# 13 node slots per tile, layer 0 projected side by side, coefficients of both layers in three column groups, 340 found tiles in layer 1

## The chip, the core and the metric

The kernel runs on one NeuronCore of a Trainium2 chip. Its engines work side by side, each through its own list of instructions, and wait for one another by semaphores: TensorE (PE, with its weight loads PEld) multiplies matrices into PSUM, VectorE (DVE) and ScalarE (ACT) work element by element, GpSimd (POOL) issues the indirect DMAs here, and SyncE (SP) issues the plain ones. The metric is the time of one execution on the device in microseconds, the median of several runs. Lower is better.

## What is computed

Two graph layers over 12500 nodes with 32 features and 200000 edges sorted by destination. Layer 0 mixes, for each edge, the source node's normalized features with nine edge values, through 32 x 32 matrices. Layer 1 mixes with 16 basis matrices whose weights depend on the edge's relation and on an attention value, plus one matrix for the last edge of each node.

```python
edge_index = jnp.stack([src, dst])
h = jnp.maximum(_layernorm(x, axis=-1), 0.0)
x = x + _L0_gnn_ref(h, edge_index, edge_weight1, edge_attr_3, edge_attr_5, L0_gnn_W)
h = jnp.maximum(_layernorm(x, axis=-1), 0.0)
x = x + _L1_gnn_ref(h, ..., src, dst, edge_type_86)
...
nei = jax.ops.segment_sum(a[:, None] * msg, dst, num_segments=N)
h_new = jnp.where((in_deg > 0)[:, None], nei + curr, jnp.zeros_like(nei))
```

Both layers sum their edge messages by destination node. Since the destination sum and the matrices commute, the kernel sums the coefficient-weighted source rows first and multiplies by the matrices afterwards.

## The kernel before

The edges are cut into tiles of 128 (one edge per partition) and the tiles into groups of 12 (`J`), 130 full groups (`FULL`) and a tail of 3 tiles. Each layer runs over the 131 groups once (`edge_sums`, `edge_copies`, `edge_work`, `edge_gathers`, `edge_loads`, one per engine); further passes over everything run only where a tile of 128 edges reaches over more destination nodes than it has slots (`WN`, 14 before).

Source rows reach SBUF (`xg`, four buffers, one per group modulo 4) in two ways. GpSimd gathers most tiles with one indirect DMA each (L564); it may begin the gathers of a group only when the sums of the group four before it are done (`summed`). The last two or three tiles of a group (`NP`, per layer and group) are found by TensorE instead: VectorE writes 0/1 blocks of the wanted row numbers (`block_rows`, L1024), TensorE multiplies them with the whole node table in 14 matmuls (`find_rows`, L636), and VectorE picks the row out of each block (`pick_rows`, L1033 and L1038). A group therefore has 12 minus `NP` gathers. Layer 0 finds 2 tiles in the first 8 groups and 3 after that. Layer 1 finds 2, then alternately 3 and 2, 322 in all.

The sums: VectorE spreads each edge's coefficients over the node slots, `Z` (`spread`, L1095; 9 coefficients in layer 0, 17 in layer 1, times 14 slots). TensorE multiplies each tile's rows with its Z (`sum_edges`, L717), in column groups of 32 (`QS`: three groups of 3 coefficients in layer 0; four groups of 5, 4, 4 and 4 coefficients in layer 1), which write to different partitions of PSUM (`G_ps`). A float32 matmul stands in the trace as two records. ScalarE copies the result to SBUF (`copy_G`, L880, L878).

The projection: in layer 0, `project` (L662) multiplies each half's three chunks with `w0c`, 64 columns wide: 32 columns of sums and 32 of the same minus their mean over the features, which the next layer's normalization uses. In layer 1 there are two steps. `project_in_quarters` (L675) writes the products of five chunks into four column groups, ScalarE copies them (`copy_oT`, L886), and `sum_quarters` (L687) adds the quarters. Then ScalarE copies the result (`copy_o`, L893), TensorE moves it to its place in the window of 128 nodes (`place_rows`, L699), and VectorE adds the window to `aggT` (`add`, L1106). Layer 1 also has attention: one-hot rows on ScalarE (L846, L850) and 36 matmuls (`attention_rows`, L649).

The order on each engine is written out by hand in the functions `step`. On TensorE, a step with new group s finds its first tile, projects group s-2, finds the other tiles, in layer 1 sums the quarters of s-2 and does the attention of s, and then sums the edges of s-1; after the first four tiles of these sums it places s-2. On VectorE a step writes blocks, picks rows and adds the window of s-3, then nodes, the first tile of s, the blocks of its third tile, and spread. On ScalarE it copies G, then (layer 1) one-hots, the quarters, attention, then placing, and last the projected rows. GpSimd does nothing but gathers.

## Time and profile before

| | us |
|---|---|
| three runs | 4622.65, 4632.38, 4634.9; median 4632.38 |
| the profiled execution | 4637.38 |
| its span, first to last instruction | 4635.5 |
| TensorE, busy | 3578.4 (77%) |
| VectorE, busy | 2689.9 (58%) |
| GpSimd, busy | 2301.7 (50%) |
| ScalarE, busy | 1097.0 (24%) |

The time of a matmul record is its start and a modelled end; the runs of records of one line are merged in the timelines. "Idle before" names what ended an engine's wait: an engine and line, "issue" where the profile shows nothing that it waited for, and "remote" for an unknown queue or a signal whose sender had been done for long.

### The profile page before, as it was taken

Reading aid. Unit: us, or ns where it says so; the run is one execution under the profiler, and the core shown is the slowest. Engines: PE = TensorE matmul, PEld = TensorE weight load, DVE = VectorE, ACT = ScalarE, POOL = GpSimd, SP = SyncE. Lnnn points to the kernel's source line nnn. Section 1 sums busy time; section 2 is a strip of 40 time slices with the busy share of each in tenths; the row PEclk is TensorE's granted clock in tenths of the full one; section 3 lists DMA queues with packets and bytes.
Section 4 is the critical chain, followed back from the end, with each engine's and each line's share of the span. In section 5 each row is a group of like instructions: output and inputs, shape, how many; then the busy total and the mean of one; then the engine's idle time right before and its main releaser. Section 6 shows DMA issues by size and latency. Waiting matters only on the chain.

```text
span 4635.5 us, 106735 instructions
## 1 busy us (share of the span) xinstructions
PE 3578.4 (77%) x41254; PEld 3052.1 (66%) x41254; DVE 2689.9 (58%) x3863; ACT 1097.0 (24%) x2563; POOL 2301.7 (50%) x2427
## 2 busy tenths in 40 slices
PE   3788888888888888885677777777777777777777
PEld 2677777777777777775566666666666666666666
DVE  5455555555555555555555665656656665556565
ACT  1111111111111111112233333333333333333332
POOL 5555555555555555553344444544444444445442
PEclk9889988888988989997788888888888888888887
DMA  3111111111111111111122222222222222222221
GB/s 102 21 21 20 20 21 19 20 20 21 20 20 21 20 20 21 21 20 54 35 38 39 38 37 38 40 37 37 37 41 37 38 39 38 37 37 39 39 37 35
DMA packets 216608, 150.09 MB, mean 32 GB/s; under 512 B 121048, under 2 KB 197261, under 8 KB 216079
## 3 DMA queue, kind: packets, MB, share of 16 engines
q0 software_dynamic: 77504, 39.84, 8.9%
q1 hardware_dynamic: 137999, 100.77, 8.8%
q8 instruction: 335, 5.49, 0.5%
q10 hardware_dynamic: 576, 2.40, 0.1%
q14 instruction: 194, 1.59, 0.1%
HBM read 134.58 MB, written 8.22 MB: 31 GB/s over the span
## 4 chain that ended last, share of the span: by engine, by line
PE 38%; issue 13%; another core or an unknown queue 2%; DVE 1%; ACT 1%; ACTq 0%; DVEq 0%
PE ps L636 20%; PE ps L717 7%; PE ps L649 5%; PE ps L675 2%; PE ps L699 1%; PE ps L687 1%; PE ps L599 0%; ACT p_left L846 0%; PE ps L619 0%; DVE room L1095 0%; DVE row_var L969 0%; ACT p_left L886 0%; DVE squares L996 0%; DVE H L966 0%
## 5 line engine op out<-in xcount | busy, mean ns | idle before, releaser
L564 POOL DMA_INDIRECT xg<-h_table,idx x2422 | 2290.8, 946 | 2272.7 <-PE ps L717 1530.1
L636 PE MATMUL ps<-h,blocks 128*128 128x448 f32 x9856 | 2284.3, 388 | 43.3 <-DVE blocks L1024 29.2
L636 PEld LDWEIGHTS ps<-h,blocks 128*128 128x128 f32 x9856 | 1937.9, 202 | 262.8 <-issue 76.6
L1024 DVE TENSOR_TENSOR blocks<-scratch,ps 128x896 fp32r<-128x896 int16 x704 | 761.2, 1082 | 882.8 <-remote 864.7
L717 PE MATMUL ps<-room,xg 128*32 128x42 f32 (+2 forms) x21882 | 699.4, 267 | 301.5 <-issue 297.4
L717 PEld LDWEIGHTS ps<-room,xg 128*32 128x32 f32 x21882 | 579.6, 144 | 429.0 <-issue 412.4
L1033 DVE SCALAR_TENSOR_TENSOR scratch<-ramp_sb,scratch,ps 128x448 f32<-128x448 f32 x704 | 476.4, 677 | 512.1 <-remote 250.7
L649 PE MATMUL ps<-att_tab,p_left 128*128 128x49 bf16 x4689 | 261.2, 200 | 555.3 <-issue 553.7
L1095 DVE TENSOR_TENSOR room<-coef,ps 128x756 f32<-128x756 f32 (+1 forms) x522 | 648.9, 1284 | 4.9 <-DVE ps L1044 0.2
L649 PEld LDWEIGHTS ps<-att_tab,p_left 128*128 128x128 bf16 x4689 | 201.6, 107 | 610.5 <-issue 609.5
L880 ACT ACTIVATE p_left<-ps 96x504 f32<-96x504 f32 (+2 forms) x262 | 168.8, 644 | 1200.8 <-PE ps L717 1200.7
L1038 DVE TENSOR_REDUCE xg<-scratch 128x32 f32<-128x448 f32 x704 | 436.6, 620 | 25.6
L893 ACT ACTIVATE p_left<-ps 84x128 f32<-84x128 f32 (+2 forms) x262 | 64.4, 246 | 1428.9 <-remote 1189.8
L846 ACT ACTIVATE p_left<-rows_b,node_all 128x512 bf16<-128x512 int16 x391 | 251.6, 705 | 48.8 <-PE ps L649 48.8
L699 PE MATMUL ps<-squares,p_left 84*64 84x128 f32 (+1 forms) x1044 | 241.3, 372 | 11.5 <-issue 10.6
L850 ACT ACTIVATE p_left<-p_left 128x1536 bf16<-128x1536 bf16 x131 | 193.5, 1477 | 4.1
L1076 DVE TENSOR_TENSOR coef<-ps,att 128x192 f32<-128x192 f32 x131 | 46.6, 356 | 232.8 <-issue 116.1
L865 ACT ACTIVATE squares<-ramp_sb,place 84x128 f32<-84x128 f32 x522 | 179.2, 391 | 9.7 <-issue 9.7
L1106 DVE TENSOR_TENSOR aggT<-aggT,ps 64x128 f32 (+1 forms) x262 | 74.1, 283 | 179.8 <-PE ps L699 137.2
L699 PEld LDWEIGHTS ps<-squares,p_left 84*64 84x64 f32 (+1 forms) x1044 | 144.4, 166 | 26.0 <-issue 13.0
L878 ACT ACTIVATE p_left<-ps 32x168 f32<-32x168 f32 x131 | 39.2, 300 | 476.9 <-PE ps L717 476.9
L662 PEld LDWEIGHTS ps<-w0c,p_left 96*84 96x84 f32 x1566 | 137.5, 155 | 11.3 <-ACT p_left L880 1.6
(108 smaller groups left out, 1144.5 us busy)
## 6 DMA issues: line engine op xcount, KB each, us to landing
xg<-h_table,idx POOLq DMA_INDIRECT x2422
rows_b<-typ_short SPq DMA_DIRECT2D x130, 258.0 KB
scratch<-q_short SPq DMA_DIRECT2D x260, 96.0 KB
rows_b<-dst_short SPq DMA_DIRECT2D x130, 126.0 KB
coef<-in_edge_dram SPq DMA_DIRECT2D x130, 54.0 KB
att_tab<-p_table SPq DMA_DIRECT2D x393, 8.1 KB
p_table<-room SPq DMA_DIRECT2D x8, 297.0 KB
X<-in_x_dram SPq DMA_DIRECT2D x7, 224.0 KB, 4.3
```

Source lines behind the costliest of these rows:

```text
L564: pool.indirect_dma_start(xg[:, g.q, t - g.s * J, :], None, h_table[n], bass.IndirectOffsetOnAxis(ap=idx[:, t:t + 1], axis=0)).then_inc(L. ...
L636: last = pe.matmul(found_ps[b], blocks[:, b, c, :], h_2[:, a, c], start=(c == 0 and a == 0), stop=(c == NCH - 1 and a == 1))
L649: last = pe.matmul(to, one_hot[:, j, :], att_tab[:, g.b, j // JS, a, :], start=(a == 0), stop=(a == 2))
L699: last = pe.matmul(win_ps[OUT[n]], o_sb[0:w, h, 0:no], R[0:w, g.b, h, :], start=(h == 0), stop=(h == hh - 1), tile_position=(0, OUT[n].start))
L717: last = pe.matmul(bank[q * F:(q + 1) * F, 0:qs[q + 1] - qs[q], j % JH, :], xg[:, g.q, j, :], Z[:, g.b, j, qs[q] * WN:qs[q + 1] * WN], sta ...
L846: act.activation(one_hot[:, js, :].rearrange("p j e -> p (j e)"), rows_b[:, b, js.start * P:js.stop * P], ACT.Abs, bias=node, scale=-1.0). ...
L850: act.activation(one, one, ACT.Relu, bias=1.0, scale=-1.0).then_inc(L.one_hot_set, 1)
L865: act.activation(R[0:w, g.b, h, :], iota_row[0:w, :], ACT.Abs, bias=at, scale=-1.0)\
L1024: dve.tensor_tensor(blocks[:, b], q_b[:, g.b, i, :].unsqueeze(1).broadcast_to([P, NCH, P]), block_ps.unsqueeze(2).broadcast_to([P, NCH, P] ...
L1033: dve.scalar_tensor_tensor(out=picked, in0=iota_row[:, 0:MC].unsqueeze(1).broadcast_to([P, F, MC]), scalar=place_in_block[:, bass.ds(u, 1) ...
L1038: dve.tensor_reduce(xg[:, g.q, j, :], picked, AX_X, ALU.add).then_inc(L.picked, 1)
L1095: dve.tensor_tensor(Z[:, b, js, 0:C * WN].rearrange("p j (c n) -> p j c n", n=WN), coef[:, js, :].unsqueeze(3).broadcast_to([P, k, C, WN]) ...
```

## The change

Tiles get 13 node slots instead of 14, so Z, the sums and all that is copied and projected shrink by a fourteenth. The 17 coefficients of layer 1 go into three column groups of 6, 6 and 5 instead of four, so there are six chunks (the last with two groups) for the projection instead of five. Layer 0 uses the two-step projection of layer 1 (`project_in_quarters`, then ScalarE's `copy_oT`, then `sum_quarters` after the second found tile) with `w0c` 32 columns wide; the centred half is no longer a product of the matmul but is made by VectorE in a new function `centre`, for which `place_rows` of layer 0 waits. In layer 1 two of three groups find 3 tiles, 340 in all.

```diff
-WN = 14
+WN = 13
-NP = [[2 if s < 8 else 3 for s in range(FULL)], [2 if s < 8 else 3 if s == FULL - 1 else 3 - s % 2 for s in range(FULL)]]
+NP = [[2 if s < 8 else 3 for s in range(FULL)], [2 if s < 8 or s == FULL - 2 else [2, 3, 3][s % 3] for s in range(FULL)]]
-QS = [[0, 3, 6, 9, 9], [0, 5, 9, 13, 17]]
-CQ = [3, 5]
-NQ = [3, 4]
+QS = [[0, 3, 6, 9, 9], [0, 6, 12, 17, 17]]
+CQ = [3, 6]
+NQ = 3
+CHUNK = [[3 * F, 3 * F, 3 * F], [3 * F, 3 * F, 3 * F, 3 * F, 3 * F, 2 * F]]
...
-                def project(g):
-                    ...
-                            last = pe.matmul(o_ps[0:w, h, 0:no], G_sb[0:rows, c, h, 0:w], weights[0:rows, c, :],
-                                             start=(c == 0), stop=(c == cq - 1))
...
                     for c in range(cq):
-                        rows, q = (P, c) if c < MQ else (F, 0)
+                        rows, q = CHUNK[n][c], c % MQ
                         last = pe.matmul(oT_ps[q * F:(q + 1) * F, 0:hh * w], weights[0:rows, c, :], G_sb[0:rows, c, 0:hh, 0:w],
-                                         start=(c < MQ), stop=(c > 0), tile_position=(0, q * F))
+                                         start=(c < MQ), stop=(c + MQ >= cq), tile_position=(0, q * F))
...
                 def place_rows(g):
-                    pe.wait_ge(L.o_set, g.order())
+                    pe.wait_ge(L.centred if n == 0 else L.o_set, g.order())
...
                 def step(gs):
                     tiles = gs[0].found_tiles(n) if gs[0] else []
                     find_rows(tiles[0:1])
+                    if gs[2]:
+                        project_in_quarters(gs[2])
+                    find_rows(tiles[1:2])
                     if n == 0 and gs[2]:
-                        project(gs[2])
-                    if n == 1 and gs[2]:
-                        project_in_quarters(gs[2])
-                    find_rows(tiles[1:])
+                        sum_quarters(gs[2])
+                    find_rows(tiles[2:])
                     if n == 1 and gs[2]:
                         sum_quarters(gs[2])
...
                 def step(gs):
                     if gs[2]:
                         copy_G(gs[2])
                     if n == 1 and gs[0]:
                         one_hots(gs[0])
-                    if n == 1 and gs[2]:
+                    if gs[2]:
                         copy_oT(gs[2])
...
+                def centre(g):
+
+                    hh, w = g.halves()
+                    dve.wait_ge(L.o_set, g.order())
+                    wait(dve, L.centred, g.order() - 1)
+                    dve.tensor_reduce(o_sum[0:w, 0:hh], o_sb[0:w, 0:hh, 0:F], AX_X, ALU.add).then_inc(L.o_sum_set, 1)
+                    dve.wait_ge(L.o_sum_set, g.order())
+                    wait(dve, L.placed, g.order() - 1)
+                    dve.scalar_tensor_tensor(out=o_sb[0:w, 0:hh, F:2 * F], scalar=-1.0 / F, op0=ALU.mult, op1=ALU.add,
+                                             in0=o_sum[0:w, 0:hh].unsqueeze(2).broadcast_to([w, hh, F]),
+                                             in1=o_sb[0:w, 0:hh, 0:F]).then_inc(L.centred, 1)
...
                     if old:
                         spread(old)
+                    if n == 0 and gs[2]:
+                        centre(gs[2])
```

## Rows read from the trace of the kernel before

**Rows 1.** The page, part 2: granted TensorE clock, tenths of full speed, 40 equal slices.

```profile
PEclk9889988888988989997788888888888888888887
```

**Rows 2.** Groups by line, 1000 to 1500 us: shapes, count | busy, mean ns | idle before.

```profile
L564 POOL DMA_INDIRECT xg<-h_table,idx x282 | 266.1, 944 | 237.7 <-PE ps L717 161.6 <-issue 76.2
...
L1024 DVE TENSOR_TENSOR blocks<-scratch,ps 128x896 fp32r<-128x896 int16 x94 | 101.5, 1079 | 170.5 <-remote 170.5
```

**Rows 3.** Groups by line, 3000 to 3500 us, the same columns.

```profile
L893 ACT ACTIVATE p_left<-ps 84x64 f32<-84x64 f32 x27 | 5.9, 219 | 172.2 <-remote 172.2
```

**Rows 4.** Timeline of TensorE in layer 0: start us, us, engine, line [idle before].

```profile
1207.76 4.21 PE L636 MATMUL ps<-h,blocks 128*128 128x448 f32 x14
1211.81 1.04 PE L662 MATMUL ps<-w0c,p_left 96*84 96x64 f32 x12
1212.67 5.92 PE L636 MATMUL ps<-h,blocks 128*128 128x448 f32 x28
1218.52 0.28 PE L717 MATMUL ps<-room,xg 128*32 128x42 f32 x6
...
1221.41 0.44 PE L717 MATMUL ps<-room,xg 128*32 128x42 f32 x16 [1.20 <-issue]
1221.78 0.65 PE L699 MATMUL ps<-squares,p_left 84*64 84x128 f32 x4
1222.36 0.80 PE L717 MATMUL ps<-room,xg 128*32 128x42 f32 x48
1223.33 3.07 PE L636 MATMUL ps<-h,blocks 128*128 128x448 f32 x14 [0.17 <-DVE scratch L1033]
```

**Rows 5.** Timeline of GpSimd in layer 0, one row per gather.

```profile
1208.62 0.94 POOL L564 DMA_INDIRECT xg<-h_table,idx  x1 [4.86 <-PE ps L717]
...
1218.61 0.95 POOL L564 DMA_INDIRECT xg<-h_table,idx  x1 [0.30 <-issue]
1223.97 0.94 POOL L564 DMA_INDIRECT xg<-h_table,idx  x1 [4.41 <-PE ps L717]
```

**Rows 6.** Timelines of ScalarE and VectorE in layer 0, the same group.

```profile
1215.75 0.27 ACT L893 ACTIVATE p_left<-ps 84x128 f32<-84x128 f32 x1 [6.19 <-remote]
...
1221.51 1.09 DVE L1024 TENSOR_TENSOR blocks<-scratch,ps 128x896 fp32r<-128x896 int16 x1 [5.33 <-remote]
```

**Rows 7.** Timeline of GpSimd in layer 1: the first gather of three groups.

```profile
3019.61 0.94 POOL L564 DMA_INDIRECT xg<-h_table,idx  x1 [7.03 <-PE ps L717]
...
3037.46 0.94 POOL L564 DMA_INDIRECT xg<-h_table,idx  x1 [6.92 <-PE ps L717]
...
3056.69 0.94 POOL L564 DMA_INDIRECT xg<-h_table,idx  x1 [7.06 <-PE ps L717]
```

**Rows 8.** Timeline of TensorE in layer 1, parts of two groups.

```profile
3028.66 0.42 PE L687 MATMUL ps<-four_units,p_left 128*84 128x32 f32 x4
...
3032.44 1.13 PE L649 MATMUL ps<-att_tab,p_left 128*128 128x49 bf16 x30 [1.22 <-issue]
...
3054.17 1.70 PE L717 MATMUL ps<-room,xg 128*32 128x56 f32 x54
3055.80 3.56 PE L636 MATMUL ps<-h,blocks 128*128 128x448 f32 x14
```

**Rows 9.** Timeline of ScalarE in layer 1, the first of these groups.

```profile
3032.73 0.22 ACT L893 ACTIVATE p_left<-ps 84x64 f32<-84x64 f32 x1 [6.94 <-remote]
```

**Rows 10.** Timeline of TensorE at the end of layer 1, after the last gather.

```profile
4583.18 0.95 PE L717 MATMUL ps<-room,xg 128*32 128x56 f32 x54
4584.06 3.10 PE L636 MATMUL ps<-h,blocks 128*128 128x448 f32 x14
4587.09 0.89 PE L675 MATMUL ps<-p_left,w_sb 128*32 128x168 f32 x10
4587.90 5.96 PE L636 MATMUL ps<-h,blocks 128*128 128x448 f32 x28
```

**Rows 11.** Groups by line, whole span: a small reduce in the setup.

```profile
L1251 DVE TENSOR_REDUCE w_sum<-w0c 128x3 f32<-128x96 f32 x1 | 0.3, 254 | 0.0
```

More of the change, by code:

```diff
@@ L385, in __init__ @@
                     self.coef_in = [sem(f"coef_in{n}_{b}") for b in range(2)]
+                    self.o_sum_set = sem(f"o_sum_set{n}")
+                    self.centred = sem(f"centred{n}")
                 if n == 1:
@@ L650, in attention_rows @@
                     last.then_inc(L.ex_done, 1)
-                def project(g):
-                    hh, w = g.halves()
-                    pe.wait_ge(L.G_set, g.order())
-                    wait(pe, L.o_set, g.order() - 1)
-                    wait(pe, L.added, g.order() - 1)
-                    for h in range(hh):
-                        for c in range(cq):
-                            rows = NQ[n] * F
-                            last = pe.matmul(o_ps[0:w, h, 0:no], G_sb[0:rows, c, h, 0:w], weights[0:rows, c, :],
-                                             start=(c == 0), stop=(c == cq - 1))
-                    last.then_inc(L.turned, 1)
                 def project_in_quarters(g):
@@ L685, in sum_quarters @@
                     pe.nop().then_inc(L.turn_go, 1)
+                    rows = min(cq, MQ) * F
                     for h in range(hh):
-                        last = pe.matmul(o_ps[0:w, h, 0:no], oT_sb[:, h, 0:w], four_units[:], start=True, stop=True)
+                        last = pe.matmul(o_ps[0:w, h, :], oT_sb[0:rows, h, 0:w], four_units[0:rows, :], start=True, stop=True)
                     last.then_inc(L.turned, 1)
@@ L715, in sum_edges @@
                         bank = G_ps[:, j // JH, 0:cq * HW].rearrange("p (c j n) -> p c j n", c=cq, j=JH)
-                        for q in range(NQ[n]):
+                        for q in range(NQ):
                             last = pe.matmul(bank[q * F:(q + 1) * F, 0:qs[q + 1] - qs[q], j % JH, :], xg[:, g.q, j, :],
@@ L761, in _ @@
             last.then_inc(q_turned, 1)
[L762 removed]
+            pe.wait_ge(w0_set, 1)
             pe.wait_ge(pw_set, 1 + MQ)
@@ L827, in edge_copies @@
                 cq = CQ[n]
-                no = OUT[n].stop - OUT[n].start
                 def attention(g):
@@ L876, in copy_G @@
                     to = G_sb[:, 0:cq, 0:hh, 0:w].rearrange("p c h w -> p h c w")
-                    if n == 1:
-                        act.activation(to[0:F, :, cq - 1, :], bank[0:F, :, cq - 1, 0:w], ACT.Copy)
-                    chunks, rows = min(cq, MQ), NQ[n] * F
-                    act.activation(to[0:rows, :, 0:chunks, :], bank[0:rows, :, 0:chunks, 0:w], ACT.Copy).then_inc(L.G_set, 1)
+                    whole = CHUNK[n].count(NQ * F)
+                    if whole < cq:
+                        rows = CHUNK[n][whole]
+                        act.activation(to[0:rows, :, whole, :], bank[0:rows, :, whole, 0:w], ACT.Copy)
+                    rows = NQ * F
+                    act.activation(to[0:rows, :, 0:whole, :], bank[0:rows, :, 0:whole, 0:w], ACT.Copy).then_inc(L.G_set, 1)
                 def copy_oT(g):
@@ L885, in copy_oT @@
                     wait(act, L.turned, g.order() - 1)
-                    act.activation(oT_sb[:, 0:hh, 0:w], oT_ps[:, 0:hh * w].rearrange("p (h w) -> p h w", h=hh),
+                    rows = min(cq, MQ) * F
+                    act.activation(oT_sb[0:rows, 0:hh, 0:w], oT_ps[0:rows, 0:hh * w].rearrange("p (h w) -> p h w", h=hh),
                                    ACT.Copy).then_inc(L.oT_set, 1)
```

18 lines of the change are left out of this document (6 added, 12 removed).

## The prediction

> **What bounds the kernel now.** I read the edge loops first: the loop of layer 0 runs from about 93 to 2110 us, that of layer 1 from about 2237 to 4597 us, 131 groups each. TensorE looks like the bound (busy 77% of the span), and in neither loop does it stand idle for long. The view by lines shows another pace. In 500 us of layer 0 GpSimd issues 282 gathers [rows 2], at 9 a group 31.3 groups, so 15.96 us a group. In layer 1 two groups that follow each other take 37.08 us, 18.5 us each [rows 7]. GpSimd is busy half of the time and its idle half ends with the line of the sums, L717.
>
> Next the timelines of one group. In layer 0 GpSimd starts nine gathers at 1208.62, 0.86 us after TensorE left the sums at 1207.76 [rows 4], one each 1.25 us, the last at 1218.61 for 0.95 us [rows 5]. Meanwhile TensorE runs 14 matmuls that find a tile (L636), the projection (L662), 28 more of L636, and begins the sums at 1218.52 [rows 4]. Then it nearly stops: single matmuls, 0.5 to 1.2 us apart, until 1221.41, when it runs on at full pace. Nothing that it waits for in the code is late: the gather that it needs was issued three groups earlier. 1221.41 is 1.85 us after the end of the last gather. In the same instant VectorE gets a signal that TensorE had raised long before (the middle tile found), after 5.33 us of waiting [rows 6]; in the 500 us this wait "remote" stands 31 times with 170.5 us [rows 2]. I call 1221.41 the release. After it come the rest of the sums, the placing (L699) and 48 more matmuls of sums, and only the last of them lets GpSimd start the next nine gathers at 1223.97 [rows 4, 5].
>
> Layer 1 is the same: L687 ends at 3029.1, the matmuls of L649 stall, the release is at 3032.44 [rows 8], and ScalarE, which waits for L687, starts only at 3032.73 [rows 9]; 172.2 us in 27 groups have that cause [rows 3]. The test that tells the pacemaker: the group from 3019.61 has 9 gathers and lasts 17.85 us; the next has 10 gathers and, by the alternation in `NP`, one found tile less, and lasts 19.23 us [rows 7]. One gather more costs about its 1.25 us, one tile (14 matmuls, about 2.9 us) less saves nothing. So a group lasts 0.8 us, its gathers at 1.25 us each, 1.9 to 2.2 us to the release, and **what TensorE has to do after the release**. Work before the release is free up to the stall (about 2.8 us in rows 4, 3.4 us and more in rows 8).
>
> **The change part by part.** The extra passes over all edges run if a tile of 128 edges reaches over more nodes than it has slots. In the inputs drawn here the widest tile reaches over 12, so they stay away with 13 slots too.
>
> Layer 0, projection. L662 (12 matmuls, 1.04 us [rows 4]) goes; in come 6 matmuls like L675, whose ten take 0.89 us [rows 10], so 0.3 to 0.5, and 4 like L687 (0.42 [rows 8]), after the second found tile. All lies before the release, under 2.8 us of stall: 0. ScalarE gets one copy more of about 0.3 us. If its signal comes late TensorE waits before the four, at most 1 to 2 us, also in the stall.
>
> One rule speaks against this part: the Trainium skill (TensorEngine Tiling (Array Packing), Tiling Modes, Key Properties) says that a change of the tiling mode drains TensorE, and layer 0 now changes to 128x32 and back in each group. By the trace L675 in column groups runs from 4587.09 for 0.89 us and L636 starts at 4587.90, with no hole [rows 10]. With a drain of some 0.1 us before the release the sum stays as it is.
>
> Layer 0, centring: **this is the term that decides**. Before, the projection wrote sums and centred sums at once, and L699 followed at 1221.78, 0.37 us after the release. Now L699 must wait for a chain: the signal of L687 (`turned`), the copy on ScalarE (L893), a reduce and a subtraction on VectorE (`centre`). L687 will be raised some 7 us after the last sum, when in layer 1 every such signal was held until the release [rows 8, 9]; and in layer 0 the tile signal raised just ahead of it was held too [rows 6]. So the chain begins at the release: arrival after 0.10 (as VectorE in rows 6) to 0.29 us (as ScalarE in rows 9), the copy 0.22 [rows 9], two VectorE operations of at most 0.25 each (a reduce of 96 elements takes 0.254 [rows 11]; these have 64), and three hand-overs, 0.05, 0.03 and about 0.15 (0.17 is VectorE to TensorE in rows 4). That is 0.94 to 1.26 us after the release instead of 0.37: +0.57 to +0.89, taken as +0.65, because the signal has only one ahead of it. Queued behind L699 on TensorE are the 48 matmuls whose last one starts the gathers, so it is paid in full: 127 paced groups x 0.65 = +83 us (72 to 113). On VectorE `centre` also stands ahead of L1024 for the next tile, which starts about 0.9 us later; the next L636 then starts some 0.4 us after the sums, which eats stall and no time.
>
> Narrower slots. L717 streams coefficient x slot columns in column groups side by side. In layer 1 (widest group 5 x 14 = 70) the 54 matmuls from 3054.17 to 3055.80 take 241 ns per tile of 8 at the lower level (1.2 GHz), and from 4583.18 to 4584.06 130 ns at 2.4 GHz [rows 8, 10]: 3.4 and 1.9 ns a column. Layer 0 goes from 42 to 39 columns: 3 x 1.9 to 3.4 ns x 10 tiles behind the release = 0.06 to 0.10 us, x 127 = -10 us. Layer 1 goes from four groups of 70, 56, 56, 56 to three of 78, 78, 65. There are 24 matmuls fewer, but the widest group grows by 8 columns: 15 to 27 ns a tile, all 12 tiles behind the release, 0.18 to 0.33 us. The granted clock is below full in most slices of this loop [rows 1], and the stretch after the stall in rows 8 runs at the lower level, so 0.30: x 129 = +39 us (23 to 43).
>
> 340 instead of 322 found tiles: 18 gathers fewer, 18 x 1.25 = -22 us; 18 x 2.9 us of TensorE work lies in stalls. TensorE reaches about 60 matmuls a group before it stalls in all of these timelines (14+12+28+6; 14+10+28+4 and six of L649); two more of L675 and the added tiles push a few L649 behind the release, at 37 ns each (30 in 1.13 us [rows 8]): +5 us (0 to 12).
>
> The rest of the edit (two operations fewer in the setup, VectorE's spread L1095 7% shorter, a copy of 780 instead of 672 elements on ScalarE under the first found tile) has engines that wait anyway: 0. The last two groups of layer 0 show the longer chain openly: +2 us.
>
> Clock. In layer 0 the granted clock is nine tenths [rows 1], and where it is high the sums after the release are short. TensorE will now idle 0.65 us more just there. If 0 to 40% of the groups turn to the lower level, 10 tiles x 42 columns x 1.5 ns = 0.63 us each: 0 to +32, taken as +10.
>
> Sum: 83 - 10 + 39 - 22 + 5 + 2 + 10 = +107 on the profiled execution's 4637 us, so 4744. The median of the three runs lies 5 us under that execution: **4739 us, +2.3%**, given as 4740. With the ends of the terms this case alone spans 4700 to 4790.
>
> **The rivals.**
> (A) `turned` of layer 0 gets through before the release. For it: L662's signal, raised at 1212.85, did reach ScalarE at 1215.75, while gathers ran [rows 6], only late, and L636 work follows L687 here as it did L662. Against: the tile signal raised ahead of it does not get through [rows 2, 6]. Then L699 doesn't wait and neither VectorE nor the clock changes: 4637 - 10 + 39 - 22 + 7 = 4651, less 5: 4646, the edge of no change. It decides from the point where the chain of about 0.9 us ends 0.4 us after the release.
> (B) The sums are bound by the number of matmuls, not by columns. At 2.4 GHz 54 take 0.88 us, 16 ns each; at 1.2 GHz 30 ns each. Were that a cost each, 24 fewer would save 0.4 to 0.7 us a group, about -75 instead of +39: 4740 - 114 = 4626, no change; with (A) as well, near 4530 and faster. Against it: the same matmuls nearly double when the clock halves, which an issue cost would not.
> The Trainium skill (TensorE: Matmul & The Clock Gate, Part 1) states that two matmuls never start less than about 25 ns apart however few their columns; by it layer 1 would gain 24 x 25 ns = 0.6 us a group. The 16 ns in rows 10 speak against it here.
> (C) The extra waits and the later L636 exhaust the stall of 2.8 us in layer 0, or the clock stays at the lower level after every release. Half a us more in each of 127 groups: 4800 and above.
> (D) The change doesn't do what it says (18 gathers fewer bring nothing because another wait paces layer 1): +22, 4762, inside the range.
>
> **How the numbers follow.** Forecast with its bounds, (D) in it: 66%. (A) 11%, (B) 7%, (A) with (B) 4%, (C) 12%. The time is the forecast's, 4740. Leaving out (C) and (A) with (B), and half of (B), leaves out about 2 in 10: 4640 to 4800. About 0.3% (14 us) is what a measurement of this kernel can tell from no change: faster 0.06, same 0.14, slower 0.80.
>
> **What would show it.** In layer 0, L699 should start 0.9 to 1.3 us after the release with a wait for VectorE's centring ahead of it, and L893 at the release and not before; gathers per 500 us fall from 282 to about 271. In layer 1 L717 should have 78 columns and take about 265 ns a tile at the lower clock; a group of 9 gathers should last about 18.2 us whether it has 2 or 3 found tiles. I am wrong if L893 of layer 0 runs while gathers still run, if L717 in layer 1 gets shorter, or if the release no longer follows the last gather by about 2 us.

## The result, and the profile after

On the chip where the kernel before takes 4632.35 us (median of four runs) the changed kernel takes 4773.76 us, 4773.19 to 4777.45: a ratio of 1.031, 95% interval 1.029 to 1.033. The forecast was 4740. The profiled execution has a span of 4775.6 us, 140.1 more than before. The page, parts 1 and 2; the clock row answers to [rows 1]:

```profile
PE 3744.1 (78%) x38384; PEld 3146.6 (66%) x38384; DVE 2732.6 (57%) x4177; ACT 1135.2 (24%) x2694; POOL 2283.3 (48%) x2409
...
PEclk8788888888888888887788888888888888888887
```

Layer 0 is slices 2 to 18. In four of them TensorE's clock stood at nine tenths before and in the others at eight; now none stands at nine, and one at seven. Groups by line of the changed kernel, 1000 to 1500 us, with the columns of [rows 2]:

```profile
L567 POOL DMA_INDIRECT xg<-h_table,idx x275 | 259.4, 943 | 242.7 <-PE ps L707 168.0 <-issue 74.7
L1017 DVE TENSOR_TENSOR blocks<-scratch,ps 128x896 fp32r<-128x896 int16 x91 | 98.0, 1077 | 8.6 <-issue 8.6
L689 PE MATMUL ps<-squares,p_left 78*64 78x128 f32 x120 | 25.7, 353 | 14.9 <-DVE p_left L1101 14.9
L886 ACT ACTIVATE p_left<-ps 78x64 f32<-78x64 f32 x30 | 6.6, 219 | 218.0 <-remote 218.0
L1098 DVE TENSOR_REDUCE o_sum<-p_left 78x2 f32<-78x64 f32 x30 | 6.5, 216 | 159.1 <-ACT p_left L886 159.1
```

GpSimd (L567 was L564) issues 275 gathers where it issued 282: at nine a group 16.4 us for a group instead of 15.96. The wait named remote has moved from VectorE's L1024 in [rows 2] to ScalarE's copy of o_ps (L886, was L893): 218.0 us in 30 groups, 7.3 us each. VectorE's centring (L1098, L1101) waits for that copy, and TensorE's placing (L689, was L699) for the centring, 14.9 us in 30 groups.

One group of layer 0 in the timelines of TensorE, ScalarE, VectorE and GpSimd, columns as in [rows 4]; it answers to [rows 4 to 6]:

```profile
1215.02 0.40 PE L677 MATMUL ps<-four_units,p_left 96*78 96x32 f32 x4
1215.26 3.08 PE L639 MATMUL ps<-h,blocks 128*128 128x448 f32 x14
1218.27 0.33 PE L707 MATMUL ps<-room,xg 128*32 128x39 f32 x9
...
1220.99 0.20 PE L707 MATMUL ps<-room,xg 128*32 128x39 f32 x1 [1.19 <-issue]
1221.70 0.40 PE L707 MATMUL ps<-room,xg 128*32 128x39 f32 x13 [0.51 <-issue]
1222.65 0.87 PE L689 MATMUL ps<-squares,p_left 78*64 78x128 f32 x4 [0.56 <-DVE p_left L1101]
1223.45 1.26 PE L707 MATMUL ps<-room,xg 128*32 128x39 f32 x48
...
1221.78 0.22 ACT L886 ACTIVATE p_left<-ps 78x64 f32<-78x64 f32 x1 [8.29 <-remote]
...
1222.04 0.22 DVE L1098 TENSOR_REDUCE o_sum<-p_left 78x2 f32<-78x64 f32 x1 [6.24 <-ACT p_left L886]
1222.29 0.22 DVE L1101 SCALAR_TENSOR_TENSOR p_left<-o_sum,p_left 78x64 f32<-78x64 f32 x1
...
1218.87 0.94 POOL L567 DMA_INDIRECT xg<-h_table,idx  x1 [0.30 <-issue]
1225.52 0.94 POOL L567 DMA_INDIRECT xg<-h_table,idx  x1 [5.71 <-PE ps L707]
```

L677 (was L687) is done at 1215.4. ScalarE gets its signal at 1221.78, 0.08 us after the release at 1221.70, which again lies 1.9 us behind the last gather. Placing starts 0.95 us after the release where it started after 0.37, and the next gathers start as before 0.8 us after the last sum. The last 48 sums took 0.80 us in [rows 4] and 1.26 here: this burst ran at the lower level (granted clock 0.50, where the one in [rows 4] had 1.00).

Layer 1, TensorE, parts of two groups, answering to [rows 8]:

```profile
3025.32 0.40 PE L677 MATMUL ps<-four_units,p_left 128*78 128x32 f32 x4
3026.98 0.18 PE L652 MATMUL ps<-att_tab,p_left 128*128 128x49 bf16 x1 [1.26 <-issue]
3029.10 1.62 PE L652 MATMUL ps<-att_tab,p_left 128*128 128x49 bf16 x35 [1.94 <-issue]
...
3050.17 1.94 PE L707 MATMUL ps<-room,xg 128*32 128x65 f32 x40
3052.04 3.32 PE L639 MATMUL ps<-h,blocks 128*128 128x448 f32 x14
```

35 of the 36 matmuls of L652 (was L649) stand behind the release, 30 did in [rows 8]. Forty sums take 1.87 us from start to start, 280 ns a tile of six, where a tile of eight took 241.

Where the 140.1 us are, by the start of the first and the end of the last sum in each layer: layer 0 +95.0 (forecast +85), between the layers +2.9, layer 1 +43.9 (forecast +22; its 126 paced groups grew by 49, the rest of it shrank by 5), the ends -1.7. Worked out from the gathers and sums of both traces, the mean time from one group's last sum to the next's, in us, with the number of groups:

```
found tiles, gathers    before            after
layer 0: 3, 9           15.90  (120)      16.61  (120)
layer 1: 3, 9           17.85  (60)       18.45  (40)
layer 1: 2, 9                             18.20  (40)
layer 1: 2, 10          19.15  (64)       19.48  (6)
layer 1: 3, 10                            19.98  (40)
```

One thing more stands in the trace after and not in the one before: in layer 1, eleven times, a gather starts 2.7 us after the one ahead of it in its group instead of 1.25, with no wait that the profile names. That is 16 us of GpSimd's time. The groups with such a gather last 0.7 to 0.8 us longer than the others of their kind, about 8 us in all; why these gathers are late is open.

### The profile page after: what moved, and what is told of

It reads as the page before. It is cut to its first block, busy times and chain, and to the rows that moved or that the text cites. A ratio compares the mean times of both kernels' runs of the same rounds, so it can differ in the third digit from the quotient of the medians.

```text
span 4775.6 us, 102031 instructions
## 1 busy us (share of the span) xinstructions
PE 3744.1 (78%) x38384; PEld 3146.6 (66%) x38384; DVE 2732.6 (57%) x4177; ACT 1135.2 (24%) x2694; POOL 2283.3 (48%) x2409
## 4 chain that ended last, share of the span: by engine, by line
PE 36%; issue 11%; another core or an unknown queue 4%; ACT 2%; DVE 1%; ACTq 0%; DVEq 0%
PE ps L639 18%; PE ps L707 7%; PE ps L652 5%; PE ps L664 2%; PE ps L689 1%; PE ps L677 1%; ACT p_left L836 1%; PE ps L602 1%; ACT p_left L879 0%; PE ps L622 0%; ACT p_left L872 0%; DVE room L1088 0%; DVE row_var L962 0%; DVE squares L989 0%
## 5 line engine op out<-in xcount | busy, mean ns | idle before, releaser
L567 POOL DMA_INDIRECT xg<-h_table,idx x2404 | 2272.4, 945 | 2438.8 <-PE ps L707 1685.6
L639 PE MATMUL ps<-h,blocks 128*128 128x448 f32 x10108 | 2419.5, 395 | 59.8 <-DVE blocks L1017 30.5
L639 PEld LDWEIGHTS ps<-h,blocks 128*128 128x128 f32 x10108 | 2014.8, 205 | 319.5 <-issue 97.6
L707 PE MATMUL ps<-room,xg 128*32 128x39 f32 (+2 forms) x18756 | 716.2, 272 | 232.8 <-issue 228.9
L1026 DVE SCALAR_TENSOR_TENSOR scratch<-ramp_sb,scratch,ps 128x448 f32<-128x448 f32 x722 | 488.0, 676 | 356.7 <-PE ps L639 174.0
L1088 DVE TENSOR_TENSOR room<-coef,ps 128x702 f32<-128x702 f32 (+1 forms) x522 | 606.5, 1203 | 5.3 <-issue 0.5
L652 PE MATMUL ps<-att_tab,p_left 128*128 128x49 bf16 x4689 | 256.2, 209 | 417.1 <-issue 415.7
L652 PEld LDWEIGHTS ps<-att_tab,p_left 128*128 128x128 bf16 x4689 | 211.9, 113 | 459.9 <-issue 457.2
L1098 DVE TENSOR_REDUCE o_sum<-p_left 78x2 f32<-78x64 f32 x131 | 28.3, 216 | 674.0 <-ACT p_left L886 642.3
L886 ACT ACTIVATE p_left<-ps 78x64 f32<-78x64 f32 (+1 forms) x262 | 57.3, 219 | 1493.4 <-remote 1483.5
L879 ACT ACTIVATE p_left<-ps 96x156 f32<-96x156 f32 (+2 forms) x262 | 77.8, 297 | 1057.2 <-remote 461.0
L689 PE MATMUL ps<-squares,p_left 78*64 78x128 f32 (+1 forms) x1044 | 254.1, 391 | 89.9 <-DVE p_left L1101 81.5
L872 ACT ACTIVATE p_left<-ps 96x468 f32<-96x468 f32 (+2 forms) x262 | 177.9, 679 | 398.0 <-PE ps L707 398.0
L689 PEld LDWEIGHTS ps<-squares,p_left 78*64 78x64 f32 (+1 forms) x1044 | 160.2, 180 | 108.7 <-issue 103.5
L677 PEld LDWEIGHTS ps<-four_units,p_left 96*78 96x78 f32 (+1 forms) x1044 | 112.3, 155 | 163.5 <-issue 149.8
L677 PE MATMUL ps<-four_units,p_left 96*78 96x32 f32 (+1 forms) x1044 | 112.9, 231 | 128.9 <-issue 85.5
```

The lines of the kernel that those rows point to most:

```text
L567: pool.indirect_dma_start(xg[:, g.q, t - g.s * J, :], None, h_table[n], bass.IndirectOffsetOnAxis(ap=idx[:, t:t + 1], axis=0)).then_inc(L. ...
L639: last = pe.matmul(found_ps[b], blocks[:, b, c, :], h_2[:, a, c], start=(c == 0 and a == 0), stop=(c == NCH - 1 and a == 1))
L652: last = pe.matmul(to, one_hot[:, j, :], att_tab[:, g.b, j // JS, a, :], start=(a == 0), stop=(a == 2))
L677: last = pe.matmul(o_ps[0:w, h, :], oT_sb[0:rows, h, 0:w], four_units[0:rows, :], start=True, stop=True)
L689: last = pe.matmul(win_ps[OUT[n]], o_sb[0:w, h, 0:no], R[0:w, g.b, h, :], start=(h == 0), stop=(h == hh - 1), tile_position=(0, OUT[n].start))
L707: last = pe.matmul(bank[q * F:(q + 1) * F, 0:qs[q + 1] - qs[q], j % JH, :], xg[:, g.q, j, :], Z[:, g.b, j, qs[q] * WN:qs[q + 1] * WN], sta ...
```

## The experiments

They ran on three chips, and this is the surprise of the case. On chips 12 and 13 the kernel before takes 3152 to 3159 us, on chip 8 4631 us, as on the chip of the result. Each ratio is to the kernel before on the same chip.

### The other chips: the two kernels themselves

No edit: the kernel before, for its trace, and the changed kernel, on chip 12. They ran in the second series, after the four of chip 13 that stand further down.

> The kernel before itself, for its trace on this chip. Two chips have been seen: on the one it takes 4632 us, and TensorE stands still in each group of tiles until about 2 us after the group's last gather; on the one of the first four experiments 3152 us, with TensorE at full clock throughout. Theory H (the difference is the hold): at 3152 us a group of layer 0 lasts about 11.4 us with L717, L699 and the next L636 back to back, and the gathers of L564 follow each other at 1.25 us without a wait for the sums; at 4632 us the group lasts 15.9 us as in rows 4 and 5. Rival (the difference is the clock alone): the same standstill is seen at 3152 us, only shorter.

> The changed kernel itself, beside the kernel before on this chip. If this chip is one on which the kernel before takes about 4632 us: ratio 1.031 as measured (4774). If it is one on which it takes 3152 us: theory H says that layer 0's new chain for placing is hidden there (L689 stands behind sums that are still running), so that what is left is TensorE's own work: l0_old's 3174 us and about 0.06 us in each of 127 groups, as between the variant with the folded centring (group of layer 0 11.40 us) and l0_old (11.33 us): 3182 us, 3174 to 3200, ratio 1.0095. Rival (the chain of copy and centring costs its 0.65 us in every group anyway): 3174 + 83 = 3257 us, ratio 1.033.

Before 3159.9 us in the profiled execution, 3158.6 median. The changed kernel 3202.2 us (3201.0 to 3204.2), ratio 1.0136 (1.0119 to 1.0153). The kernel before on chip 12, TensorE and GpSimd in layer 0:

```profile
805.71 0.80 PE L717 MATMUL ps<-room,xg 128*32 128x42 f32 x48
806.44 3.10 PE L636 MATMUL ps<-h,blocks 128*128 128x448 f32 x14
809.38 1.04 PE L662 MATMUL ps<-w0c,p_left 96*84 96x64 f32 x12
810.24 5.92 PE L636 MATMUL ps<-h,blocks 128*128 128x448 f32 x28
816.08 0.50 PE L717 MATMUL ps<-room,xg 128*32 128x42 f32 x24
816.52 0.65 PE L699 MATMUL ps<-squares,p_left 84*64 84x128 f32 x4
...
806.06 0.95 POOL L564 DMA_INDIRECT xg<-h_table,idx  x1 [0.30 <-issue]
807.32 0.94 POOL L564 DMA_INDIRECT xg<-h_table,idx  x1 [0.30 <-issue]
```

The same instructions with the same durations as in [rows 4, 5] (5.92 us for 28 L636, 1.04 for L662, 1.25 from gather to gather), but nothing stands still: TensorE goes from one line to the next at full clock, GpSimd issues gather after gather, and a group takes 11.5 us instead of 15.9. Theory H holds, the clock alone doesn't make the difference. The changed kernel there:

```profile
802.90 0.40 PE L677 MATMUL ps<-four_units,p_left 96*78 96x32 f32 x4
803.14 3.13 PE L639 MATMUL ps<-h,blocks 128*128 128x448 f32 x14
806.20 0.48 PE L707 MATMUL ps<-room,xg 128*32 128x39 f32 x24
806.61 0.65 PE L689 MATMUL ps<-squares,p_left 78*64 78x128 f32 x4
...
803.34 0.22 ACT L886 ACTIVATE p_left<-ps 78x64 f32<-78x64 f32 x1 [1.93 <-PE ps L677]
...
803.64 0.21 DVE L1098 TENSOR_REDUCE o_sum<-p_left 78x2 f32<-78x64 f32 x1
803.88 0.22 DVE L1101 SCALAR_TENSOR_TENSOR p_left<-o_sum,p_left 78x64 f32<-78x64 f32 x1
```

The signal of L677 starts ScalarE within 0.1 us; the centring is done at 804.1, 2.5 us before placing, which waits for nothing. Layer 0 comes out even, 1460 us from its first to its last sum before and 1461 after; layer 1 goes from 1521 to 1566. Even is the sum of two things: l0_old below, which has all of the change but the new projection, has a layer 0 of 1440 us (chip 13), so 13 slots save some 20 us there and the new projection costs them again. The expectation (3174 to 3200) was missed by 2 us, its rival (3257) by far. The chain behind the release, the term that decided the forecast, is paid only where TensorE's signals come late.

### Layer 0's change alone

The kernel before with `project` and its 64 columns replaced as in the change: 14 slots, 322 tiles, four groups in layer 1.

```diff
-                    if n == 0 and gs[2]:
-                        project(gs[2])
+                    if gs[2]:
+                        project_in_quarters(gs[2])
+                    find_rows(tiles[1:2])
+                    if n == 0 and gs[2]:
+                        sum_quarters(gs[2])
...
+                    if n == 0 and gs[2]:
+                        centre(gs[2])
```

> The kernel before with the change's layer 0 alone: three chunks side by side, their sum, the 32-column copy and the centring by VectorE; 14 slots, 322 found tiles and layer 1 as before. On a chip of 4632 us: the chain behind the release costs 0.71 us in each of 127 groups (as the two traces show), +90 us, 4722, 4700 to 4740; rival (the 0.71 us is layer 1's or the clock's): under +30 us. On a chip of 3152 us: +5 to +12 us, as nothing waits for the centring (3160, 3150 to 3170); rival (the chain costs there too): +80 us, 3235.

Chip 12: 3174.3 us, ratio 1.0051 (1.0034 to 1.0068), +15.7 us where +5 to +12 was forecast. Its span grew by 11.2; layer 0 alone grew by 13, a group of it from 11.47 to 11.55 us in the mean. Some 7 of the 13 us stand in the ten groups at the turn of the loop, where TensorE now waits 0.7 us for VectorE's pick (L1026), which stands behind the centring in VectorE's list; before it did not wait there. The rest is spread over the other groups.

### The change without layer 0's new projection

```diff
-                    if gs[2]:
-                        project_in_quarters(gs[2])
-                    find_rows(tiles[1:2])
-                    if n == 0 and gs[2]:
-                        sum_quarters(gs[2])
+                    if n == 0 and gs[2]:
+                        project(gs[2])
```

> The changed kernel with layer 0's projection and centring as before (one step, 64 columns, no centring on VectorE); 13 slots, three column groups and 340 found tiles stay. Theory (the chain signal, copy, centring on VectorE stands between the release and the placing): the groups of layer 0 fall from 16.6 to about 15.8 us, the kernel from 4774 to about 4670 us, and the placing starts 0.35 to 0.4 us after the release. Rival (the clock or the narrower slots make layer 0 longer): it stays within 20 us of 4774.

Chip 13, where the kernel before takes 3152.0 us: 3174.0, ratio 1.0071 (1.0055 to 1.0086). The expectation counted on the standstill, which this chip doesn't have, so it tells nothing of it; it tells that the rest of the change costs 22 us on such a chip. The expectations of the next three runs (folded, 340 tiles, 13 slots) were likewise written for the slower kind, and their figures could not be tested.

### Centring folded into a constant

The changed kernel with the last matmuls 64 columns wide (the second 32 subtract the mean) and no work for VectorE.

```diff
-            dve.tensor_tensor(four_units[:], two_units[:, 0:F], two_units[:, F:2 * F], ALU.add).then_inc(units_set, 1)
+            dve.tensor_tensor(four_units[:, 0:F], two_units[:, 0:F], two_units[:, F:2 * F], ALU.add).then_inc(units_set, 1)
+            dve.wait_ge(units_set, 2)
+            dve.tensor_scalar(four_units[:, F:2 * F], four_units[:, 0:F], -1.0 / F, None, ALU.add).then_inc(units_set, 1)
...
-                    if n == 0 and gs[2]:
-                        centre(gs[2])
```

> The changed kernel, but the centring is folded into the constant matrix of the quarter sums (units minus 1/32 in a second half of 32 columns), so VectorE has no part in it; the two-step projection and its place stay. Theory: the chain behind the release shrinks to signal, copy and hand-over, so the placing starts about 0.55 us after the release instead of 0.95, 0.4 us x 127 groups = 50 us less, about 4722 us. If VectorE's part is not what costs and the two-step projection itself does (late signals, waits before the quarter sums), it stays near 4774; if all of the extra wait is VectorE's, it falls by 75 or more.

Chip 13: 3198.7 us, ratio 1.0145 (1.0129 to 1.0160). Inconclusive for the same reason. Against l0_old it is 25 us slower: 12.1 in layer 0 (11.40 instead of 11.32 us a group), so the new projection costs something even without VectorE's part, and 12.5 in layer 1, where every twelfth group, the one at the turn of the loop, takes about 11.8 us instead of 10.4 though its code does the same. TensorE waits there 0.65 us for ScalarE's copy of G and 0.34 for VectorE's Z, in l0_old for neither. The changed kernel on chip 12 has the same two waits in the same group. Why they come is open.

### 340 found tiles alone, 13 slots alone

```diff
-NP = [[2 if s < 8 else 3 for s in range(FULL)], [2 if s < 8 else 3 if s == FULL - 1 else 3 - s % 2 for s in range(FULL)]]
+NP = [[2 if s < 8 else 3 for s in range(FULL)], [2 if s < 8 or s == FULL - 2 else [2, 3, 3][s % 3] for s in range(FULL)]]
```

> The kernel before with 340 instead of 322 found tiles in layer 1 and nothing else. Theory after the result: 18 gathers less give 22 us, but TensorE reaches about 60 matmuls before it stalls, so in the groups that find 3 tiles nearly all of the attention matmuls stand behind the release, 0.3 to 0.4 us more in each; 20 groups more of that kind and the other 60 unchanged from before: 4632 - 22 + 8 = 4618 us. Rival A (added tiles are fully hidden): 4610. Rival B (each added tile is paid, or late signals in groups with 3 tiles and 10 gathers cost 0.5 us each): 4630 or above.

```diff
-WN = 14
+WN = 13
```

> The kernel before with 13 slots instead of 14 and nothing else. Theory (sums behind the release are bound by the columns of the widest group): layer 1's widest group falls from 70 to 65 columns, 5 x 1.9 to 3.4 ns x 12 tiles x 129 = 15 to 26 us, layer 0 from 42 to 39, 10 us: 4600 us, 0.7% faster. Rival (bound by the number of matmuls): within 8 us of 4632.

Chip 13: 340 tiles 3187.7 us, ratio 1.0115 (1.0099 to 1.0130); 13 slots 3135.6 us, 0.9949 (0.9935 to 0.9963), the only version faster than before. GpSimd's gathers by line in layer 1, 1750 to 3000 us, with the columns of [rows 2]: before and changed (chip 12), then 340 tiles and 13 slots (chip 13), each from its own view:

```profile
L564 POOL DMA_INDIRECT xg<-h_table,idx x1000 | 946.0, 946 | 305.0 <-issue 305.0
```

```profile
L567 POOL DMA_INDIRECT xg<-h_table,idx x962 | 910.1, 946 | 340.9 <-issue 289.6 <-PE ps L707 51.2
```

```profile
L564 POOL DMA_INDIRECT xg<-h_table,idx x966 | 911.5, 944 | 338.6 <-issue 291.2 <-PE ps L717 47.4
```

```profile
L564 POOL DMA_INDIRECT xg<-h_table,idx x1002 | 945.7, 944 | 305.4 <-issue 305.4
```

Before, GpSimd never waits for the sums: 1000 gathers x 1.25 us fill the 1250. With 340 tiles it waits 47 us for them (TensorE busy 1232.5 of 1250 us): TensorE paces layer 1 now, and a tile found is 14 matmuls where a gather was 1.25 us. With 13 slots GpSimd fills its 1250 us again, so what TensorE saves in layer 1 hardly comes through (1516 us from first to last sum, 1521 before on chip 12); most of the 16 us is layer 0, 1440 instead of 1460.

### Three column groups alone

The kernel before with layer 1's 17 coefficients in groups of 6, 6 and 5.

```diff
-QS = [[0, 3, 6, 9, 9], [0, 5, 9, 13, 17]]
-CQ = [3, 5]
-NQ = [3, 4]
+QS = [[0, 3, 6, 9, 9], [0, 6, 12, 17, 17]]
+CQ = [3, 6]
+NQ = [3, 3]
```

> The kernel before with layer 1's coefficients in three column groups alone (widest 84 columns at 14 slots, 72 sum matmuls in a group of tiles where 96 stood). Theory W (a tile of sums costs by the columns of its widest group): a tile of layer 1 takes 84/70 of its time. On a chip of 4632 us: 12 tiles x 0.30 us x 14/8 of the forecast's widening from 70 to 78 would be +0.5 us in each of 129 groups, +68 us, 4700, 4670 to 4730. On a chip of 3152 us, where a record of sums took 19.4 ns with 65 columns and 28.0 ns with 78: 72 x 30 ns where 96 x 20.3 ns stood, +0.2 us in each group, +27 us, 3179, 3165 to 3195. Theory N (a tile costs by the number of its matmuls): 24 fewer in each group, 24 x 20 ns x 129 = -62 us.

Chip 12: 3161.3 us, ratio 1.0007 (0.9998 to 1.0017). Neither theory gave the time. TensorE in layer 1, the end of a group's sums, before and with three groups:

```profile
3034.37 0.98 PE L717 MATMUL ps<-room,xg 128*32 128x56 f32 x54
3035.28 3.10 PE L636 MATMUL ps<-h,blocks 128*128 128x448 f32 x14
```

```profile
3024.27 1.25 PE L718 MATMUL ps<-room,xg 128*32 128x84 f32 x41
3025.45 3.10 PE L637 MATMUL ps<-h,blocks 128*128 128x448 f32 x14
```

A tile takes 0.91 us / (54/8) = 135 ns with 70 columns and 1.18 / (41/6) = 173 with 84; the changed kernel has 151 with 78. So theory W has the duration: 1.9 to 2.1 ns a column at 2.4 GHz, with eight records a tile as with six. The time hardly moves because TensorE had the room: busy 1223.5 of 1250 us of layer 1 before, 1249.7 here.

### A standstill that is asked for

Four kernels meant to imitate the standstill on a chip without it; they ran on chip 8, which has it of its own. In each, TensorE waits ahead of the sums of group g in layer 0 until the gathers of group g+3 have landed:

```diff
+                def stand_still(g):
+                    if n == 0 and isinstance(g.k, int) and isinstance(g.s, int) and g.s + 3 < FULL:
+                        later = Group(0, g.s + 3, 0)
+                        pe.wait_ge(L.gathered[later.q], later.gathers(n) * 16)
```

The first is the kernel before, the second has layer 0's change alone, the third and fourth raise the signal for ScalarE's copy only behind the wait (`pe.wait_ge(L.side_done, back.order())`, then `pe.nop().then_inc(L.turned, 1)`), the fourth with the folded centring.

> The kernel before with one wait more for TensorE in each group of layer 0: ahead of the sums of group g it waits until the gathers of group g+3 have landed (those that GpSimd can issue before it needs these sums). This imitates, on a chip where TensorE runs through, the standstill of rows 4 and 5. Theory H: GpSimd issues 9 gathers at 1.25 us, they land some 2 us later, the sums take 1.2 us and only then GpSimd goes on: 14.5 to 15.9 us for a group of layer 0 where 11.46 stood, 3158 + 127 x 4 = 3666 us, 3540 to 3730. On a chip where the kernel before takes 4632 us the wait is nearly fulfilled when it comes: 4632 us, up to 1% more. Rival (a standstill in TensorE is taken back by the slack of the group): under 3250 us.

> The same wait in the kernel before with the change's layer 0 alone; the signal that o_ps is complete is given by the matmul itself, so that ScalarE's copy and VectorE's centring run during the standstill. Theory H (the change costs by its chain only where this signal comes at the end of the standstill): like held_before, 0 to +16 us. Rival (the chain costs 0.6 to 0.7 us in each group that stands still, whenever the signal is given): +75 to +90 us over held_before.

> As held_early, but the signal that o_ps is complete is given only at the end of the standstill (TensorE waits for its own matmuls and raises it with an instruction of its own), as the trace of the changed kernel shows it. Theory H: placing stands 0.95 us behind the release where 0.37 us stood: +0.58 us x 127 = +74 us over held_before, +60 to +95. Rival (another wait bounds the release, or 24 matmuls of sums cover the chain): 0 to +25 us.

> As held_late, with the centring folded into the constant of the last matmuls (64 columns, no work for VectorE): what is left behind the late signal is ScalarE's copy of 0.22 us. Theory H: the copy is done some 0.4 us after the release, about when the 24 matmuls ahead of placing are out (0.41 us): +5 to +20 us over held_before, some 60 us under held_late. Rival (the late signal and ScalarE's queue cost, not VectorE's two steps): within 20 us of held_late.

The kernel before 4631.3 us; held_before 4691.0 (ratio 1.0117, 1.0089 to 1.0145), held_early 4758.3 (1.0274, 1.0257 to 1.0291), held_late 4771.2 (1.0303, 1.0286 to 1.0320), held_fold 4783.2 (1.0325, 1.0300 to 1.0351). Means over the groups of layer 0, worked out from the traces (us; the release is where the sums start or go on at pace, the last column the bursts of sums at a mean clock under 0.75):

```
              group   last gather's   release      release       lower
                      end to release  to placing   to last sum   clock
before        15.90   1.90            0.38         2.26          68 of 117
after         16.61   1.95            0.91         2.92          83 of 117
held_before   16.31   1.74            0.73         2.83          87 of 117
held_early    16.78   1.89            1.00         3.17          90 of 116
held_late     16.94   2.35            0.66         2.86          96 of 115
held_fold     17.03   2.38            0.67         2.93          100 of 115
```

held_early answers the question of rival (A) by itself. Its groups by line, 300 to 1400 us:

```profile
L892 ACT ACTIVATE p_left<-ps 84x64 f32<-84x64 f32 x65 | 14.2, 219 | 476.9 <-remote 476.9
L1104 DVE TENSOR_REDUCE o_sum<-p_left 84x2 f32<-84x64 f32 x65 | 14.0, 216 | 335.7 <-ACT p_left L892 335.7
```

Here the matmul that raises the signal starts, and by its modelled end is done, some 5 us ahead of the release, and TensorE is only waiting for data. Still ScalarE's whole wait is remote, 7.3 us a group: the early signal does not come early on this chip. The trace also keeps the moment at which each semaphore is raised: between 300 and 2100 us it lies 5.4 us (median of 108 groups) behind the matmul that raises it, never while gathers run, and 2.0 us behind the last of them. In the changed kernel of the result it lies 5.3 us behind (median of 109 groups), on chip 12 0.01. So the semaphore is raised late, and ScalarE is not late to see it; whether the matmul itself really ends late can't be told, as the ends of matmuls are modelled. held_before itself came out just above the 1% that was allowed for it. My 0 to +16 us over held_before was wrong (+67), as it took for granted that a signal given early arrives early. For held_late +74 was expected and +80 came, but not by the mechanism: placing is no later than in held_before, the release is, by 0.6 us. Groups by line of held_late, 300 to 2100 us:

```profile
L720 PE MATMUL ps<-room,xg 128*32 128x42 f32 x7632 | 204.9, 258 | 316.2 <-remote 211.8 <-DMA xg<-h_table,idx 103.9 <-issue 0.4
```

In held_before the wait ahead of these sums is for the gathers alone (306.0 of 311.1 us). The wait that held_late adds is TensorE's for its own signal; that semaphore too is raised 5.6 us (median of 106 groups) behind its matmul. held_fold, forecast 60 us under held_late, lies 12 above it: with its rival. In both, placing stands 0.66 us behind the release, with VectorE's part and without. The pair doesn't settle whether folding would help the changed kernel on such a chip, as the added wait may hide the chain. Folding without it wasn't run there.

## Why the prediction was right, and where it was off

Direction and size came out, the larger part by the mechanism forecast, on a chip of the kind on which the trace of before was taken. The parts of the change weren't run singly on such a chip, so their shares below are read from the two traces; the nearest test of layer 0's part there is held_early over held_before, +67 us. The measured growth is 33 us above the forecast: 10 in layer 0, 22 in layer 1, 1 in the rest. (The prediction's own terms, all taken at their ends, reach from 4694 to 4804, a little further than the 4700 to 4790 that it states.)

Layer 0, the chain: right, and its size was nearly right. Placing stands 0.95 us after the release in the group shown (forecast 0.9 to 1.3), 0.91 in the mean of 117 groups against 0.38 before: +0.53, so 127 x 0.53 = 67 us where +83 stood. ScalarE's copy runs at the release and not before, 650.9 us of its waits in 500 to 2000 us having that cause. Rival (A) is out: the signal doesn't get through. It is the case of chips 12 and 13, where its point of decision is met by 2.5 us.

Layer 0, the clock: the term that was mis-sized downward. The prediction read the clock of layer 0 as nine tenths off [rows 1], where most slices show eight; the mean by the windows below is 0.90, so the misreading did no harm. What else the layer cost is 28 us, forecast as +10 for the clock, -10 for the columns and +2 at the ends. By the table, the release lies 0.05 us later behind the last gather (6 us), the burst from placing to the last sum is 0.13 us longer (17 us, the columns' gain already in it), and the last two groups and the start take 5. The windows of layer 0 from the first sums to the last, before and after (start and end, length, busy time and count of TensorE, its weight loads, VectorE, ScalarE and GpSimd, then TensorE's clock, the DMA share and GB/s):

```profile
93.00:2126.00 2033.00, 1714.55 (x16672) 1481.91 (x16674) 1144.83 (x1652) 240.98 (x649) 1076.49 (x1141) 0.90 0.12 20
```

```profile
93.00:2222.00 2129.00, 1781.69 (x16486) 1471.02 (x16477) 1179.01 (x1912) 269.20 (x779) 1076.42 (x1141) 0.85 0.11 19
```

The clock (third number from the end) went from 0.90 to 0.85, and 83 of 117 bursts behind the release run at a mean clock under 0.75 where 68 did. Such a burst takes 2.6 us instead of 1.8 before, 3.2 instead of 2.3 after. 15 more of them are 13% of the groups, inside the 0 to 40% of the forecast, but each costs 0.8 to 0.9 us and not 0.63, which counted only the sums and not the placing: an estimated 12 to 13 of the 17 us.

Layer 1, columns: right. 280 ns a tile at the lower clock where 265 was forecast, 151 at full clock. From a group's first sum to its last, placing included, 3.08 us became 3.31 in the mean of 126 groups: +29 us, forecast +39 (23 to 43). Rival (B) is out: on both kinds of chip fewer matmuls with wider groups take longer a tile. The 25 ns that the Trainium skill gives as the least distance of two matmuls (TensorE: Matmul & The Clock Gate, Part 1) is not seen for these matmuls in column groups: 54 records start within 0.91 us, 17 ns apart.

Layer 1, what TensorE does between the release and the sums: **the step that failed**. It was taken at +5 us, 0 to 12, for a few matmuls of L649 more behind the release at 37 ns each. Measured over the 126 paced groups of both traces, the stretch from the release to the first sum went from 0.96 to 1.19 us: +29 us. It goes by the number of found tiles:

```
                      groups   matmuls of L649/L652    release to    clock there: lower,
                               behind the release      first sum     in between, full
before, two found     66       16.6                    0.79 us       66, 0, 0
before, three found   60       31.0                    1.14          34, 6, 20
after, two found      46       18.8                    0.88          46, 0, 0
after, three found    80       31.1                    1.37          77, 2, 1
```

(The release is the first matmul behind the last hole over 0.15 us; lower is a mean clock under 0.75, full over 0.9.) Two things were priced too low. The 20 groups that went from two to three found tiles moved some 14 matmuls each behind the release, 0.58 us a group, 12 us. And in the groups with three found tiles as many stood behind it as before, but they now run at the lower clock nearly always: 0.22 us x 60 = 13 us. Why the clock fell there is open. The prediction had a clock term for layer 0 and none here. The groups with two found tiles add 4.

Gathers: 18 fewer bring their 22 us, as a gather more is worth 1.3 to 1.5 us in the table of groups, but the eleven late gathers take 16 of GpSimd's time back, so the gathers of a group end only 0.05 us earlier (-6 us). The rest of the 49, -3 us, is a shorter time from the last sum to the next first gather. That a group of 9 gathers lasts about 18.2 us with two or with three found tiles held by the medians (18.25 and 18.24), and by the means not quite (18.20 and 18.45; 18.14 and 18.37 without the groups that have a late gather). With 10 gathers the third tile costs 0.5 us, from six groups only.

The tiling mode: the prediction, seeing no hole at L675 in [rows 10], took the drain to be small or absent. The ends of matmuls are modelled, so a missing hole doesn't tell; the starts do. At full clock on chip 12 one L636 starts 203 ns after the one ahead of it, and L662 or L687, not in column groups either, 205 after the last L636, but L675, L717 and the changed kernel's L664, in column groups, 297. The change of mode is thus seen, at some 0.09 us on the way in. In layer 0 of the result it lies ahead of the release, and the 0 stands. Rival (C) didn't come: the groups of layer 0 grew by 0.71 us in the mean, not by 0.5 more than forecast. Rival (D) is out for the chip of the result by the table of groups (9 gathers instead of 10 make a group 1.3 to 1.5 us shorter), though the 340 tiles weren't run alone there; for chips 12 and 13 it is right, and more than right, as they cost 36.

What no step had: that all this holds for one kind of chip. On the other the change costs 1.4%, net nearly all in layer 1 (+45 us). By parts: 340 tiles +36, the new layer 0 +16, three groups +3, 13 slots -16, together 39 of the 44 us.

## What to carry to other kernels

When an engine stands still for nothing that it waits for, look at when its signals arrive: a wait named remote on the receiving engine, ending at the same instant as the standstill, says that any hand-over added in that stretch starts at its end and is paid in full, while work added ahead of it is free only up to what the engine gets done before it stops. Price a new hand-over by both: on a chip where the signal comes at once the same edit cost 16 us instead of the 67 of its chain, and by other waits.
A trade of one engine's work for another's (gathers for found tiles) has to be priced at the engine that paces the layer, and that engine differed between the two kinds of chip; 13 slots alone take work from TensorE and VectorE and add none to GpSimd, and were the only part that gained there, 0.5%.
Price what stands behind the release at the clock that it will have there, not at the one that a single group shows: that was the largest miss here.

## What the runs showed of the hardware

The same program takes 3152 to 3159 us on two chips and 4631 to 4632 us on two occasions elsewhere, 47% more, with equal durations of the single operations at the same granted clock. On the slower kind a signal that TensorE raises during a run of GpSimd's indirect gathers is late. The signal of L677 in layer 0 of the changed kernel is raised 5.3 us (median) behind its matmul and in none of 109 groups before the run is over; ScalarE and, in held_late, TensorE itself wait for it, and TensorE stops after some 60 matmuls. The signal of L662, raised earlier in the run, came 2.9 us late while gathers were still running [rows 6]. On the faster kind the delay is 0.01 us while gathers follow each other without end. What differs between the chips is open.
A change from the full array to column groups takes TensorE 0.09 us more from start to start than going on in the full array (297 instead of 203 to 205 ns, chip 12).
An added wait that ends about when the release comes cost 60 us there (held_before, 0.41 us a group). Kernels in which TensorE rests longer had more bursts at the lower clock, 68 before and 83 to 100 in the five others of the table; since a lower clock also makes the group longer, these runs don't separate cause and effect.
